# Filling a projection's PSUM bank in two halves: twelve products of 256 columns in place of six of 512, in a two-layer graph network kernel

## The reference

```python
# layer 0
h = relu(layernorm(x));  x = x + adj @ (h @ weight) + bias
# layer 1, with 8 heads of 256 columns
h = relu(layernorm(x))
feat_proj = (h @ fc_w + fc_b).reshape(bs, n, HEADS, dim).transpose(0, 2, 1, 3)
q = feat_proj @ q_w + q_b;  k = feat_proj @ k_w + k_b
masked = leaky_relu(q + k.T + (1 - adj) * NEG, 0.01)
out = softmax(masked) @ feat_proj
out = out.transpose(0, 2, 1, 3).reshape(bs, n, HEADS * dim) @ fp_w + fp_b + h
x = x + sigmoid(out)
```

## Time and profile before

| what | value |
|---|---|
| median of 3 runs | 1406.91 us (1406.39 to 1406.93) |
| the profiled execution's own time | 1406.65 us |
| its span, first to last instruction | 1404.9 us |
| PE busy | 99% of the span |
| VectorE busy | 91% |
| ScalarE, GpSimd busy | 80%, 78% |
| granted TensorE clock | 1.00 |

### The profile page before, as it was taken

How to read it: one execution, slowest core, us unless ns; L and a number is a source line. 1 busy time by engine, 2 the same in 40 slices (tenths; PEclk the granted TensorE clock), 3 DMA queues, 4 the chain that set the end, 5 groups by cost and what they waited for, 6 DMA issues and landing times.

```text
span 1404.9 us, 31603 instructions
## 1 busy us (share of the span) xinstructions
PE 1394.7 (99%) x9048; PEld 1252.5 (89%) x9048; DVE 1285.1 (91%) x4408; ACT 1126.5 (80%) x3429; POOL 1102.0 (78%) x1295
## 2 busy tenths in 40 slices
PE   9999999999999999999999999999999999999998
PEld 7898899899899889998998898998989989988987
DVE  7999999999999999999999999999999999998996
ACT  4878788788888888887888888888878878887876
POOL 4788878878778878778787788787787887888764
PEclk9999999999999999999999999999999999999999
DMA  7423323323223233233232232232332322322221
GB/s 238 98 63 107 107 54 106 91 69 106 71 88 106 55 105 106 54 105 97 63 106 80 79 106 61 99 106 54 105 103 58 106 88 73 106 67 85 77 61 41
DMA packets 177132, 124.69 MB, mean 89 GB/s; under 512 B 137808, under 2 KB 143568, under 8 KB 177104
## 3 DMA queue, kind: packets, MB, share of 16 engines
q1 hardware_dynamic: 176816, 124.35, 30.3%
q10 hardware_dynamic: 288, 0.01, 0.0%
HBM read 105.98 MB, written 18.35 MB: 89 GB/s over the span
## 4 chain that ended last, share of the span: by engine, by line
PE 94%; POOL 2%; issue 1%; DVE 1%; DMA 1%; ACT 0%; POOLq 0%; SPq 0%; ACTq 0%; DVEq 0%
PE gbank L381 48%; PE ybank L381 24%; PE tbank L481 8%; PE bank L381 6%; PE bank L426 4%; PE bank L462 2%; PE bank L449 2%; DMA late<-key_rows 0%; POOL att L1561 0%; POOL att L1554 0%; DMA qk<-qk_w_dram 0%; DVE att L829 0%; POOL xb L1544 0%; POOL t_pos L1546 0%; POOL ends L1577 0%
## 5 line engine op out<-in xcount | busy, mean ns | idle before, releaser
L1233 ACT ACTIVATE att<-att 128x128 f32<-128x128 f32 x1024 | 397.8, 393 | 47.0 <-DVE att L836 44.0
L381 PE MATMUL gbank<-m_hi,hT_lo 128*128 128x512 f32 x1024 | 426.7, 417 | 0.0
L1554 POOL TENSOR_TENSOR att<-late,t_pos 128x512 f32<-128x512 f32 x256 | 330.6, 1293 | 120.5 <-PE tbank L481 115.8
L381 PE MATMUL gbank<-m_hi,hT_hi 128*128 128x512 f32 x1024 | 403.2, 394 | 0.0
L381 PE MATMUL gbank<-m_lo,hT_hi 128*128 128x512 f32 x1024 | 401.3, 392 | 0.0
L812 DVE TENSOR_TENSOR g_lo<-gbank,g_hi 128x512 fp32r<-128x512 f32 x512 | 341.4, 678 | 47.1 <-ACT g_hi L1226 42.0
L1561 POOL TENSOR_TENSOR att<-att,rinv 128x512 f32<-128x512 f32 x256 | 289.4, 1131 | 107.1 <-DVE rinv L841 106.5
L1226 ACT ACTIVATE g_hi<-gbank 128x512 fp32r<-128x512 f32 x512 | 291.1, 595 | 39.6 <-PE gbank L381 39.4
L829 DVE TENSOR_SCALAR_CACHE_REDUCE att<-att,qs 128x128 f32<-128x128 f32 x1024 | 291.6, 341 | 27.0 <-POOL att L1554 26.7
L381 PE MATMUL ybank<-g_hi,pT_hi 128*128 128x256 f32 x1016 | 281.5, 277 | 0.0
L381 PE MATMUL ybank<-g_hi,pT_lo 128*128 128x256 f32 x1016 | 281.4, 277 | 0.0
(11 more groups left out here) (97 smaller groups left out, 2323.1 us busy)
## 6 DMA issues: line engine op xcount, KB each, us to landing
late<-key_rows SPq DMA_DIRECT2D x64, 1024.0 KB, 6.1
g_in<-graph_dram SPq DMA_DIRECT2D x64, 512.0 KB, 3.4
out_dram<-ends SPq DMA_DIRECT2D x63, 256.0 KB, 3.9
qs<-key_rows SPq DMA_DIRECT2D x128, 4.0 KB, 2.5
key_rows<-kq_sb SPq DMA_DIRECT2D x64, 24.0 KB, 1.4
att<-fc_wT_dram SPq DMA_DIRECT2D x4, 256.0 KB, 5.6
late<-fp_w_dram SPq DMA_DIRECT2D x4, 256.0 KB, 5.3
ends<-fp_w_dram SPq DMA_DIRECT2D x2, 512.0 KB, 7.9
```

What stands on the lines that cost most here:

```text
L381: mm = pe.matmul(out_ap, w, m, start=first and n == 0, stop=last and n == len(terms) - 1)
L1233: e = act.activation(a[:, s], a[:, s], ACT.Exp, scale=-1.0, bias=a[:, CH + h:CH + h + 1], accum_out=esum[j][c][:, h:h + 1])
L1554: gp.tensor_tensor(a, keys[q][:, j, c * HC:(c + 1) * HC, :], t_pos[q][:, j, :].unsqueeze(1).broadcast_to([P, HC, P]), ALU.add)\
```

## The change

`project` fills the bank head by head. A loop over k = 0, 1 issues the six products for the columns of one head (256) into the left and then into the right half of the bank, so a bank takes twelve products of 256 columns. The signal is given by the last of the twelve, as before by the last of the six. Results, operands, banks and the other engines' programs are the same.

```diff
-                j, s = n // GC, slice(n % GC * BANK, (n % GC + 1) * BANK)
-                split(bank[:],
-                      [((hT_hi[q][:, dt, j, :], hT_lo[q][:, dt, j, :]), (m_hi[:, dt, s], m_lo[:, dt, s]))
-                       for dt in range(DT)]).then_inc(pe_g[n], 1)
+                j = n // GC
+                for k in range(2):
+
+                    s = slice((n % GC * 2 + k) * D, (n % GC * 2 + k + 1) * D)
+                    mm = split(bank[:, k * D:(k + 1) * D],
+                               [((hT_hi[q][:, dt, j, :], hT_lo[q][:, dt, j, :]), (m_hi[:, dt, s], m_lo[:, dt, s]))
+                                for dt in range(DT)])
+                mm.then_inc(pe_g[n], 1)
```

## The result

The changed kernel takes 1435.88 us (1435.77 to 1436.53, 4 runs) against 1406.65 us before (1406.14 to 1406.93, 4 runs): slower by 29 us, a ratio of 1.0209 with a 95% interval of 1.0192 to 1.0227. The forecast was 1429.0 us, 1409 to 1444. The profiled execution took 1435.82 us.

The account below looks back on a forecast made before the run. PE's stream of products was taken to bound the kernel. Per step, a 0.52 us surcharge less a 0.17 us gain is 0.35 us; times 64, 22.4 us on 1406.65 gives 1429.0 us, range 1409 to 1444.

Parts of the forecast that it names:

- What bounds the kernel: PE's own stream of products is the time; no engine releases it late, its longest wait being 1.8 us.
- Two paces: Rows of 256-column products keep their starting pace, quick 0.1136 us or slow 0.1182 us a product.
- price of halves as such: In `project`, eight banks of twelve quick 256-column products take 10.88 us in place of 11.05, gaining 0.17 us a step.
- The queries turn a quick row slow: Behind `queries_keys`, four blocks of twelve 256-column products, 48 a step, run slow at 0.0046 us more each.
- The share of the 108 products behind 4-byte groups: Of 108 products a step in rows beginning behind 4-byte groups, 8 in 13 are slow: 66.
- all slow: Rows hand the slow pace through 4-byte groups, all 156 products a step slow: 1441.7 us, chance 0.05.
- the wide products: 512-column products in the loop separate 256-column rows from the queries and 4-byte groups; the change removes these separators.
- the surcharge: Each slow 256-column product costs 0.0046 us more; 114 slow ones make 0.52 us a step.
- the mix that it rests on: Some 48 to 150 of a step's 156 full-width 256-column products are slow, giving 1429.0 us; chance 0.77.
- The fixed cost per product: Each product brings at most 0.0069 us; 3072 more cost 21.2 us, giving 1427.9 us; chance 0.04.
- The supply of instructions: The slow pace is PE's sequencer delivering load and product pairs; quick needs a filled queue: 1464 us, chance 0.03.
- the weight loads: In `project`, twelve loads a bank in place of six, inside the pace at no extra cost; missing cover means slow.

Follow-up runs that it names:

- the probes: The kernel before with extra products behind its last one, run twice with different orders of 256- and 512-column products; 256-column spacings 0.1178 us slow, 0.1133 quick.
- first experiment: Kernel before with only banks n = 0 and n = 6 of `project` in 256-column halves: 1405.31 us against 1406.74, ratio 0.9988.
- second probe: Kernel before plus stretches of 96 256-column products, parted by 4, 3, 6, 1, 4 wide products, four narrow, 4 wide, four transposes; slow stretch 0.1178 us, quick 0.1133.
- second experiment: Kernel before with only bank n = 3, directly behind `queries_keys`, in 256-column halves: 1424.87 us against 1406.74, ratio 1.0125.
- last experiment: Kernel before, loop only: banks 0, 6 in halves; wide terms five in bank 2, four in 3, three in 5 and 7: 1405.88 us against 1406.83, ratio 0.9994.
- first probe: Kernel before plus 96-product stretches of 256 columns parted by wide, narrow or transpose products, then 24 products per other width; all nine stretches spaced 0.1178 us.

## Why the prediction was right, and where not

**What bounds the kernel** held: PE's stream of products is the time, the change brought no wait into it, the other engines had room.

**Two paces** held, with their sizes: 0.1136 and 0.1182 us a product in the prediction, 0.1133 and 0.1178 over the long stretches of the probes. That the untouched products of `attend` and `transform` would take over the pace, the part of the sum that outweighs the new ones, held in the trace after. So did the price of halves as such: a gain of 0.01 to 0.02 us a bank when quick (first experiment).

**The queries turn a quick row slow** had rested on one case. It held in the second probe, and in the second experiment a bank in halves behind them was slow. It is no rule of the queries alone, though: twice outside the loop of the changed kernel a slow row ran into them, they were quick themselves (0.1133 us), and so were the 48 products behind. The first of the two, in the chain in order of time:

```profile
118.67 1.42 PE gbank L381 x12
120.09 0.46 PE bank L462 x4
120.54 1.36 PE gbank L381 x12
```

**The share of the 108 products behind 4-byte groups** is the step that failed. I took 8 in 13 for them, as if each group drew the pace anew. In the loop all of them are slow; the case that came true is the rival *all slow*, to which I gave 0.05. Between 131 and 1318 us of the changed kernel all 270 stretches of 4-byte products between two such rows lead from a slow row to a slow one; at its ends, where PE also waits at times, 8 led from slow to quick and 11 from quick to slow. So such a stretch neither keeps a pace as such, as the rival had it, nor draws it. The loop repeats itself, and what comes out in one step comes out in every step; counting starts from the uneven ends could not give a share for it. Why it is slow behind each of the loop's groups isn't shown; that they move the alignment is only the likely reading. Behind it lay a second error: I took the wide products for what keeps rows quick. In most rows they only step through three alignments, and it is their number and the alignment at which they begin that count; halving one bank or one term lost it for most of the step.

**The size.** For all slow the prediction had 0.55 us a step and 35 us; the step grew by 0.52 (the surcharge is 0.0044 us, not 0.0046), but the whole by 29. I had counted start and end as steps of the loop. There many rows were slow already in the kernel before, and PE waits now and then: up to the eighth pair the changed kernel lost 1.4 us and behind the 60th 1.2 us; the 51 steps between gave 26.5. So the forecast of 1429.0 had some 9 us too little for these steps (0.35 us each in place of 0.52) and some 2 us too much for the 13 others (4.5 in place of 2.6). That it came within 7 us owes something to luck: the mix that it rests on did not occur in the loop, and the two errors are of opposite sign. That the waits would stay small held; the 1.8 us of the earlier trace rows are two waits together, the longer of 1.2.

**The fixed cost per product** is refuted by the first and the last experiment; the first one, with 768 products more, took 1.4 us less. The rule of the Trainium skill that the prediction quotes, N/2.4 + 2.5 ns ("TensorE: Matmul & The Clock Gate", "Back-to-back issue gap"), is given there for an isolated product. It is no guide for these rows of fp32r products with a weight load each: by it the change would cost 7.7 us, and 29 were measured. **The supply of instructions** is refuted by the probes, and so are the weight loads as the cause of the slow pace.

**What stays open** is what the alignment is against. The start times of products in the loop before, taken over 1.2 ms, cluster at a period of 6.667 ns; the quick spacing of 113.3 ns is 17 of these, the slow cycle of three (353.3 ns) 53 and the cycle 226, 229, 232 (686.7 ns) 103. So these three patterns close on such a grid. The step of the loop does too, in all twelve kernels apart from the probes: 3214 periods before (21.4267 us), 3292 in the changed kernel (21.9467 us), each within 0.05 ns of a whole number. That is a regularity of the traces, not a mechanism, and which unit keeps the grid wasn't tried. Nor is it shown what puts a row into one pace behind 4-byte groups, or wide products into the pattern of 233 ns.

## What to carry to other kernels

When a kernel is bound by TensorE's stream, look at the spacing of like products, not at their number or listed duration: products of one form can run at two paces in one trace, and an edit can change the pace of products that it doesn't touch. If a small edit on such an engine costs far more than its instructions, compare the untouched groups first. In a hardware loop a pace is not a matter of chances, since each step repeats the last: one product more or fewer ahead of a group can be tried, and it settled 25 us here; but such a gain is tied to the exact order and must be measured again after each edit.

## What the hardware showed that was not expected

- 256-column fp32r products have two stable spacings, 113.3 and 117.8 ns, at a full clock and with no wait, and hold either over 96 products.
- Two quick products of 256 columns (226.7 ns) take less than one of 512 in most long rows (229 on average, in turns of 226, 229, 232).
- A single product more in a step (last term of bank 0 in halves) moved some 1900 spacings of the loop to the slow pace.
- Spacing by width, from the slow side, third to last of 24 products each in the first probe: 111.9 ns for 224 columns, 111.9 for 232, 111.8 for 240, 113.4 for 248, 121.0 for 264, 126.7 for 272, 131.4 for 288, 146.6 for 320, 173.3 for 384, 200.0 for 448, 217.9 for 480, 226.8 for 496, 229.0 for 504. At 272, 320, 384 and 448 columns that is N/2.4 plus 13.3 ns, at 288 it is 1.9 ns less, so there is no one rule; each width was tried once. 504 columns cost as much as 512 (229).
